# A softmax denominator's inverse: VectorE's reciprocal replaced by Ln and Exp on ScalarE, in an eight-core transformer layer

## The chip, the cores and the metric

One Trainium2 chip, all 8 of its cores. Each core runs the same program on its own 2 of 16 sequences; no core talks to another. The metric is the device time of the slowest core, in microseconds (us). Two runs of the kernel before gave 9357.95 and 9133.69 us, median 9245.82 us.

## The reference

A transformer layer with a layer norm behind each half, in float32, on x of 16 x 2048 x 2048. What matters here is the attention, and in it the division by the sum of the exponentials (the rest of the layer is cut short):

```python
q = einsum('bsd,ed->bse', x, Wq)...; k = ...; v = ...      # 16 heads of 128
q = q * cos + rotate_half(q) * sin                         # k the same
scores = einsum('bhqd,bhkd->bhqk', q, k) / sqrt(128)
scores = where(causal, scores, finfo.min)
attn = softmax(scores, axis=-1)                            # exp(s) / sum(exp(s))
out = einsum('bhqk,bhkd->bhqd', attn, v) ... @ Wo.T
x = layernorm(x + out)
x = layernorm(x + (relu(relu(x @ W1.T + b1) @ W2.T + b2) @ W3.T + b3))
```

## The kernel before

The program goes through five stages for each of a core's two sequences (b = 0, 1), with a barrier of all engines ahead of the attention and behind it: Q, K and V projections (matmuls L384 and L433), attention (L498, L545, L554), output projection with the first layer norm (L660), and the three feed-forward layers (L724, L754, L790) with the second. Every instruction of an engine stands in the order in which the Python code emits it. The helpers `C.pe`, `C.act` and `C.dve` append to an engine's list, with semaphore waits written out by hand; nothing reorders them.

In the attention one unit of work is a block of 512 queries (index `q4`, 0 to 3) of one head, so there are 16 x 4 units for each sequence and 128 in all. A unit has `nci = 4*q4 + 4` blocks of 128 keys, that is 4, 8, 12 and 16 blocks for `q4` of 0, 1, 2 and 3. For each block, `emit_st` puts down:

- on TensorE the scores, 128 keys x 512 queries, into one of four PSUM banks (L498);
- on ScalarE `exp(score * scale - 16)`, PSUM to SBUF in bf16 (L512);
- on VectorE, in the last four blocks of the unit, which hold the diagonal, a memset of the masked columns (L509) and a multiplication of 128 x 128 by the triangular mask (L519).

`emit_lav` then puts down two matmuls that read the exponentials: a column of ones, which adds them up into row 0 of `l_bank` (L545), and V, which accumulates 128 x 512 in `avb` (L554). Scores run three blocks ahead of them. With `q4 = 0` all four blocks are diagonal ones, so that L545 waits for VectorE's mask from its first block on; with `q4` of 1 or more the first blocks need ScalarE alone.

At the end of a unit the sums in row 0 of `l_bank` are inverted. VectorE does it in four steps on 1 x 512 elements, of which the last three split the result into two bf16 numbers:

```python
t_rc = C.dve(... e.reciprocal(linv_sb[0:1, :], l_bank.t[0:1, :]) ...)     # L575
t_hi = C.dve(... linv_hi <- linv_sb ...)                                  # L579
t_hf = C.dve(... linv_hif <- linv_hi ...)                                 # L581
t_lo = C.dve(... linv_lo <- linv_sb - linv_hif ...)                       # L583
```

What uses them is put off by one unit. `flush_tail[0]()` (L574) emits the tail of the unit before: two matmuls that spread the inverse over 128 rows (L592, L595), a copy of it to SBUF (L600) and the multiplication with `avb` (L606), both on VectorE, and the store of the product (L612), which ScalarE's queue issues. So the order on VectorE at the end of unit n is L600 and L606 of unit n-1, then L575 to L583 of unit n, then the masks of unit n+1. On ScalarE the order is the exponentials of unit n, the store of unit n-1 (which waits for L606), then the exponentials of unit n+1.

Of the kernel before, what the change touches and what calls it, by code (L numbers as in the profile page):

```python
# [10 lines left out]
AF = mybir.ActivationFunctionType  # L11
# [126 lines left out]
def build_program(cfg, debug=False):  # L138
# [47 lines left out]
    with st:  # L186
        C = Ctx(nc, st)
        s_pe, s_act, s_dve = C.sems["pe"], C.sems["act"], C.sems["dve"]
# [3 lines left out]
                for nm in ("x0", "x1", "wq", "wk", "wv", "wo", "w1", "w2", "w3")}  # L192
# [32 lines left out]
        consts = nc.alloc_sbuf_tensor("consts", [128, 4], F32)  # L225
# [7 lines left out]
        linv_sb = nc.alloc_sbuf_tensor("linv_sb", [1, 512], F32)  # L233
        linv_hi = nc.alloc_sbuf_tensor("linv_hi", [1, 512], BF16)
        linv_hif = nc.alloc_sbuf_tensor("linv_hif", [1, 512], F32)
# [9 lines left out]
        banks = [Bank(st.enter_context(nc.psum_tensor(f"pb{i}", [128, 512], F32)))  # L245
                 for i in range(8)]

        NEGC, SCL, EPSC = 0, 1, 2
        cvec = lambda i: consts[:, i:i + 1]

        C.dve(lambda e: e.memset(consts[:, NEGC:NEGC + 1], -CSHIFT), inc=False)
        C.dve(lambda e: e.memset(consts[:, SCL:SCL + 1], SCALE), inc=False)
        C.dve(lambda e: e.memset(consts[:, EPSC:EPSC + 1], EPS), inc=False)
        C.dve(lambda e: e.memset(ones_cb[:, :], 1.0), inc=False)
        C.dve(lambda e: e.memset(ones_rb[:, :], 1.0), inc=False)
        C.dve(lambda e: e.memset(ones_rf[:, :], 1.0))
# [7 lines left out]
                       waits=[tk_ini])  # L264
# [89 lines left out]
        for b in range(B):  # L354
            if b == 0:
                C.barrier()
            for dc in range(ND):
                tk_xT = C.ld(m_xt, AA[:, xT_o + dc * S: xT_o + (dc + 1) * S],
                             xb_hbm.ap()[b, :, dc * 128:(dc + 1) * 128],
                             waits=[tk_xcast[b], (s_pe, prev_f_last)], transpose=True)  # L360
# [8 lines left out]
            for (wsrc, wtok, dst) in ((wq_bf, tk_wq, qT_hbm), (wk_bf, tk_wk, kT_hbm)):  # L369
                for h in range(H):  # L370
# [6 lines left out]
                        waits=[wtok, pan_freed[bi], (s_pe, prev_f_last)])  # L377
                    for sb in range(NSB):
                        bk = banks[it % 2]
                        for dc in range(ND):  # L380
                            wl = []
                            if dc == 0:
# [6 lines left out]
                                waits=wl, inc=(dc == ND - 1))  # L389
# [9 lines left out]
                            waits=[(s_pe, tmm), (s_dve, tmp_done[r]), tk_ini,  # L399
                                   (s_act, prev_ln_sqrt), (m_sout, m_sout.n)])  # L400
# [7 lines left out]
                            waits=[(s_dve, tc), stage_store[r]])  # L408
# [4 lines left out]
                                               waits=[(s_dve, td)])  # L413
# [5 lines left out]
            for eb in range(NEB):  # L419
# [6 lines left out]
                    waits=[tk_wv, vp_freed[bi], (s_pe, prev_f_last)])  # L426
                for sc in range(NS):
                    bk = banks[2 + (it % 2)]
                    for dc in range(ND):
                        wl = []  # L430
                        if dc == 0:
# [6 lines left out]
                            waits=wl, inc=(dc == ND - 1))  # L438
# [5 lines left out]
                        waits=[(s_pe, tmm), vs_store[r]])  # L444
# [8 lines left out]
                                        waits=[(s_act, tev)])  # L453
# [13 lines left out]
            linv_used = None  # L467
            rep_prev = None
# [4 lines left out]
            for h in range(H):  # L473
# [13 lines left out]
                for q4 in range(NSB):  # L487
                    nci = 4 * q4 + 4
                    avb = av_banks[iav[0] % 2]
                    l_bank = l_banks[iav[0] % 2]  # L490
# [76 lines left out]
                    tav_last = None  # L567
                    for ci in range(3, nci):
                        emit_st(ci)
                        tav_last = emit_lav(ci - 3)  # L570
                    tav_last = emit_lav(nci - 3)
                    tav_last = emit_lav(nci - 2)
                    tav_last = emit_lav(nci - 1)
                    flush_tail[0]()  # L574
                    t_rc = C.dve(lambda e, l_bank=l_bank: e.reciprocal(  # L575
                        linv_sb[0:1, :], l_bank.t[0:1, :]),
                                 waits=[(s_pe, tav_last), (s_dve, linv_used),
                                        (s_pe, rep_prev)])
                    t_hi = C.dve(lambda e: e.tensor_copy(linv_hi[0:1, :], linv_sb[0:1, :]),  # L579
                                 waits=[(s_dve, t_rc)])  # L580
                    t_hf = C.dve(lambda e: e.tensor_copy(linv_hif[0:1, :], linv_hi[0:1, :]),  # L581
                                 waits=[(s_dve, t_hi)])
                    t_lo = C.dve(lambda e: e.tensor_sub(linv_lo[0:1, :], linv_sb[0:1, :],  # L583
                                                        linv_hif[0:1, :]),
                                 waits=[(s_dve, t_hf)])
                    linv_used = t_lo
                    l_bank.free = (s_dve, t_rc)

                    def tail(l_bank=l_bank, avb=avb, t_lo=t_lo, tav_last=tav_last,
                             q4=q4, h=h, b=b):  # L590
# [41 lines left out]
            for g in range(NS // 4):  # L632
# [5 lines left out]
                    waits=[otg_freed[gb]])  # L638
                otg = AB[:, otg_o + gb * H * 512: otg_o + (gb + 1) * H * 512]
                for eb in range(NEB):  # L640
# [6 lines left out]
                        waits=[tk_wo, wop_freed[wb_i]])  # L647
                    for si in range(4):
# [5 lines left out]
                                          waits=[xc_freed[xr]])  # L654
                        bk = banks[itb % 6]
                        for h in range(H):
                            wl = []
                            if h == 0:
# [6 lines left out]
                                waits=wl, inc=(h == H - 1))  # L665
# [240 lines left out]
```

How the kernel before makes its waits and increments, by code:

```python
    def emit(self, eng, fn, waits=(), inc=None, inck=1):  # L76
        lst = self.ops[eng]
        wt = self.waited[eng]
        for w in waits:
            if w is None:
                continue
            s, v = w
            if v is None or v <= 0:
                continue
            if wt.get(s.name, 0) >= v:
                continue
            wt[s.name] = v
            lst.append(lambda e, s=s, v=v: e.wait_ge(s.h, v))
        if inc is not None:
            inc.n += inck
            tok = inc.n
            def run(e, fn=fn, inc=inc, k=inck):
                fn(e).then_inc(inc.h, k)
            lst.append(run)
            return tok
        lst.append(fn)
        return None
# [28 lines left out]
    def barrier(self):  # L128
        toks = [(s, s.n) for s in self.all_sems if s.name not in self.no_barrier]
        for e in self.ENGS:
            for s, v in toks:
                if v <= 0 or self.waited[e].get(s.name, 0) >= v:
                    continue
                self.waited[e][s.name] = v
                self.ops[e].append(lambda eng, s=s, v=v: eng.wait_ge(s.h, v))
# [691 lines left out]
        def final_waits(e):  # L827
            for s, v in fin:
                if v > 0:
                    e.wait_ge(s.h, v)
```

## Time and profile before

| | us |
|---|---|
| two runs | 9133.69, 9357.95 (median 9245.82) |
| profiled execution | 9160.52 |
| its slowest core, first to last instruction (the span) | 9158.9 |
| spans of the eight cores | 9042.0 to 9158.9 |
| attention stages of the slowest core | about 1822 to 2740 and 5848 to 6744 |

The profile is of the slowest core, core 1, and times in it count from the start of its span. "Busy" is time in which an engine ran an instruction; a row of the timeline that ends in brackets says how long the engine stood idle before it and what ended that. [...]

### The profile page before, as it was taken

What the parts mean: (1) busy time and instruction counts of PE and PEld (TensorE: products, weight loads), DVE (VectorE), ACT (ScalarE), POOL (GpSimd) and SP (SyncE); (2) the same over time, 40 slices, a digit from 0 to 9 for tenths busy, and PEclk for the clock granted to TensorE, in tenths of its full rate; (3) what the DMA queues carried; (4) which work ended last, traced back from release to release, by engine and by line L of the source; (5) the groups of instructions that cost most, each with busy time, mean ns of one, the idle gap of its engine ahead of it and who ended that gap; (6) DMA issues with size and microseconds to landing.
All of it is one profiled execution on the core that took longest, in us unless ns stands there. A gap on an engine that the chain in (4) does not pass through costs nothing.

```text
span 9158.9 us, 76236 instructions; the slowest of 8 cores (9042.0 to 9158.9 us)
## 1 busy us (share of the span) xinstructions
PE 6904.8 (75%) x28800; PEld 2716.3 (30%) x28800; DVE 2147.2 (23%) x3399; ACT 1432.9 (16%) x2116; POOL 33.5 (0%) x68
## 2 busy tenths in 40 slices
PE   0000099977776698998989799877766798989898
PEld 0000044411112243443434344311122343434343
DVE  0000087055542201000000474255532001010101
ACT  0000000144440110101010000344420101011010
POOL 0000000000000000000000000000000000000000
PEclk9999999978778899999999899877788999999999
DMA  9999922211116645444444422111136544444444
GB/s 116 110 109 111 119 76 87 67 37 38 37 46 212 180 149 164 149 157 160 172 150 162 120 78 82 54 44 37 38 128 204 156 159 157 159 152 149 168 146 155
DMA packets 423222, 1097.90 MB, mean 120 GB/s; under 512 B 228433, under 2 KB 277713, under 8 KB 367825
## 3 DMA queue, kind: packets, MB, share of 16 engines
q1 hardware_dynamic: 282066, 824.54, 27.4%
q0 software_dynamic: 8704, 134.22, 12.6%
q10 hardware_dynamic: 132096, 134.25, 4.5%
q8 instruction: 240, 3.93, 0.2%
q14 instruction: 116, 0.95, 0.0%
HBM read 1025.78 MB, written 268.44 MB: 141 GB/s over the span
## 4 chain that ended last, share of the span: by engine, by line
PE 63%; SPq 13%; DMA 13%; DVE 5%; issue 2%; another core or an unknown queue 1%; ACT 1%; ACTq 0%; DVEq 0%; POOLq 0%
PE pb L754 18%; SPq L112 13%; PE pb L384 10%; PE pb L724 8%; PE pb L790 6%; PE pb L554 5%; PE pb L545 5%; DMA arena_a<-w_bf 5%; PE pb L433 5%; DMA arena_b<-w_bf 4%; DMA arena_b<-wo_bf 3%; PE pb L660 3%; PE pb L498 2%; DVE linv_sb L575 1%
## 5 line engine op out<-in xcount | busy, mean ns | idle before, releaser
L384 PE MATMUL pb<-arena_a,arena_b 128*128 128x512 bf16 x4096 | 892.0, 381 | 1205.6 <-DMA arena_b<-wq_bf 1198.3
L754 PE MATMUL pb<-arena_a,arena_b 128*128 128x512 bf16 x8192 | 1770.0, 379 | 8.7 <-ACT arena_a L731 7.4
L724 PE MATMUL pb<-arena_b 128*128 128x512 bf16 x4096 | 931.4, 385 | 264.3 <-DMA arena_b<-w_bf 217.7
L754 PEld LDWEIGHTS pb<-arena_a,arena_b 128*128 128x128 bf16 x8192 | 800.4, 98 | 978.3 <-issue 15.8
L512 ACT ACTIVATE arena_b<-pb,consts 128x512 bf16<-128x512 f32 (+3 forms) x1280 | 854.1, 714 | 923.4 <-DVE ot_stage L606 460.7
L790 PE MATMUL pb<-arena_a,arena_b 128*128 128x512 bf16 x4096 | 937.4, 388 | 80.9 <-DMA arena_a<-w_bf 79.1
L803 DVE TENSOR_TENSOR farena<-pb,xc_sb 128x512 f32<-128x512 f32 x128 | 88.5, 691 | 3767.9 <-PE pb L796 3767.9
L384 PEld LDWEIGHTS pb<-arena_a,arena_b 128*128 128x128 bf16 x4096 | 402.2, 98 | 1694.8 <-issue 1216.5
L545 PE MATMUL pb<-arena_b,ones_cb 128*1 128x512 bf16 x1280 | 555.9, 434 | 376.4 <-ACT arena_b L512 188.8
L660 PE MATMUL pb<-arena_b 128*128 128x512 bf16 x2048 | 498.8, 409 | 252.7 <-DMA arena_b<-wo_bf 221.6
L724 PEld LDWEIGHTS pb<-arena_b 128*128 128x128 bf16 x4096 | 393.7, 99 | 800.8 <-issue 374.3
L790 PEld LDWEIGHTS pb<-arena_a,arena_b 128*128 128x128 bf16 x4096 | 398.5, 100 | 589.7 <-issue 155.0
L554 PE MATMUL pb<-arena_b 128*128 128x512 bf16 x1280 | 570.6, 446 | 0.0
L498 PE MATMUL pb<-arena_b 128*128 128x512 bf16 x1280 | 501.4, 444 | 21.4 <-DMA arena_b<-v_hbm 21.4
L397 DVE TENSOR_TENSOR farena<-pb,sin_sb 64x512 f32<-64x512 f32 x256 | 177.3, 693 | 1171.3 <-PE pb L384 1170.6
L433 PE MATMUL pb<-arena_b,arena_a 128*128 128x512 bf16 x2048 | 442.7, 379 | 1.0 <-ACT v_stage L442 1.0
L575 DVE RECIPROCAL linv_sb<-pb 1x512 f32<-1x512 f32 x128 | 426.8, 3335 | 4.9 <-PE pb L554 4.9
L761 ACT ACTIVATE arena_b<-pb,b2t_sb 128x512 bf16<-128x512 f32 x256 | 175.9, 687 | 1603.4 <-PE pb L754 1603.4
L323 ACT ACTIVATE farena<-farena 128x2048 f32<-128x2048 f32 x64 | 122.2, 1910 | 1814.1 <-DVE farena L803 1053.3
L545 PEld LDWEIGHTS pb<-arena_b,ones_cb 128*1 128x1 bf16 x1280 | 101.2, 79 | 966.1 <-issue 966.1
L660 PEld LDWEIGHTS pb<-arena_b 128*128 128x128 bf16 x2048 | 210.7, 104 | 541.7 <-issue 337.6
L731 ACT ACTIVATE arena_a<-pb,b1t_sb 128x512 bf16<-128x512 f32 x256 | 175.8, 687 | 862.6 <-PE pb L724 853.4
(53 smaller groups left out, 2271.6 us busy)
## 6 DMA issues: line engine op xcount, KB each, us to landing
arena_b<-w_bf SPq DMA_DIRECT2D x256, 1024.0 KB, 4.9
arena_b<-w_bf SPq DMA_DIRECT2D x256, 512.0 KB, 3.4
arena_a<-w_bf SPq DMA_DIRECT2D x32, 4096.0 KB, 15.2
arena_b<-wo_bf SPq DMA_DIRECT2D x32, 2048.0 KB, 10.9
w_bf<-w2T POOLq DMA_DIRECT2D x8, 4096.0 KB, 787.3
xc_sb<-x SPq DMA_DIRECT2D x128, 256.0 KB, 5.2
y_hbm<-farena ACTq DMA_DIRECT2D x32, 1024.0 KB, 8.9
xc_sb<-y_hbm SPq DMA_DIRECT2D x128, 256.0 KB, 4.6
```

Of the source, the lines that this page charges most:

```text
L112: fn = lambda e: e.dma_start(out, in_, transpose=True)
L384: tmm = C.pe(lambda e, bk=bk, off=off, dc=dc, sb=sb: e.matmul(bk.t[:, :], AB[:, off + dc * 128: off + (dc + 1) * 128], AA[:, xT_o + dc * S ...
L433: tmm = C.pe(lambda e, bk=bk, off=off, dc=dc, sc=sc: e.matmul(bk.t[:, :], AA[:, xT_o + dc * S + sc * 128: xT_o + dc * S + sc * 128 + 128], ...
L498: tmm = C.pe(lambda e, bk=bk, ci=ci, q4=q4, qb=qb, kb=kb: e.matmul(bk.t[:, :], kb[:, ci * 128:(ci + 1) * 128], qb[:, q4 * 512:(q4 + 1) * 512],
L512: te = C.act(lambda e, bk=bk, ao=ao, j=max(j, 0): e.activation(AB[:, ao + 128 * j: ao + 512], bk.t[:, 128 * max(j, 0):], AF.Exp, bias=cvec ...
L545: C.pe(lambda e, ci=ci, ar=ar, l_bank=l_bank: e.matmul(l_bank.t[0:1, :], ones_cb[:, :], AB[:, ab_o + ar * 512: ab_o + (ar + 1) * 512], sta ...
L554: tav = C.pe(lambda e, ci=ci, ar=ar, avb=avb, vb=vb: e.matmul(avb.t[:, :], vb[:, ci * 128:(ci + 1) * 128], AB[:, ab_o + ar * 512: ab_o + ( ...
L575: t_rc = C.dve(lambda e, l_bank=l_bank: e.reciprocal(linv_sb[0:1, :], l_bank.t[0:1, :]), waits=[(s_pe, tav_last), (s_dve, linv_used), (s_p ...
L660: tmm = C.pe(lambda e, bk=bk, h=h, si=si, woff=woff, otg=otg: e.matmul(bk.t[:, :], otg[:, h * 512 + si * 128: h * 512 + si * 128 + 128], A ...
L724: tmm = C.pe(lambda e, bk=bk, woff=woff, dc=dc: e.matmul(bk.t[:, 0:STILE], AB[:, woff + dc * 128: woff + (dc + 1) * 128], AB[:, yT_o + dc ...
L754: tmm = C.pe(lambda e, bk=bk, woff=woff, ec=ec: e.matmul(bk.t[:, 0:STILE], AB[:, woff + ec * 128: woff + (ec + 1) * 128], AA[:, h1_o + ec ...
L790: C.pe(lambda e, bk=bk, woff=woff, ec=ec, si=si: e.matmul(bk.t[:, :], AB[:, h2_off(ec) + si * 128: h2_off(ec) + si * 128 + 128], AA[:, wof ...
```

## The change

The inverse of the sum l is no longer VectorE's reciprocal but exp(-ln(l)), in two ScalarE activations of 1 x 512 elements: Ln from PSUM into `linv_hif` (which serves as scratch and is overwritten by L581 later), then Exp with a scale of -1, read from a new column of `consts`, into `linv_sb`. VectorE's three remaining steps wait for ScalarE in place of VectorE. Both activations stand in ScalarE's queue where the code stood for VectorE: behind the store that `flush_tail` issues, ahead of the exponentials of the next unit. `l_bank` is now freed by Ln.

```diff
-        NEGC, SCL, EPSC = 0, 1, 2
+        NEGC, SCL, EPSC, NEG1 = 0, 1, 2, 3
...
+        C.dve(lambda e: e.memset(consts[:, NEG1:NEG1 + 1], -1.0), inc=False)
...
                     flush_tail[0]()
-                    t_rc = C.dve(lambda e, l_bank=l_bank: e.reciprocal(
-                        linv_sb[0:1, :], l_bank.t[0:1, :]),
-                                 waits=[(s_pe, tav_last), (s_dve, linv_used),
-                                        (s_pe, rep_prev)])
+                    t_ln = C.act(lambda e, l_bank=l_bank: e.activation(
+                        linv_hif[0:1, :], l_bank.t[0:1, :], AF.Ln),
+                        waits=[(s_pe, tav_last), (s_pe, rep_prev),
+                               (s_dve, linv_used)])
+                    t_rc = C.act(lambda e: e.activation(
+                        linv_sb[0:1, :], linv_hif[0:1, :], AF.Exp,
+                        scale=consts[0:1, NEG1:NEG1 + 1]),
+                        waits=[(s_act, t_ln)])
                     t_hi = C.dve(lambda e: e.tensor_copy(linv_hi[0:1, :], linv_sb[0:1, :]),
-                                 waits=[(s_dve, t_rc)])
+                                 waits=[(s_act, t_rc)])
...
                     linv_used = t_lo
-                    l_bank.free = (s_dve, t_rc)
+                    l_bank.free = (s_act, t_ln)
```

The line numbers of the changed kernel are higher by 1 up to this place and by 5 behind it: L512 becomes L513, L579 becomes L584, L606 becomes L611.

ScalarE, from the last two exponentials of a unit with `q4 = 3` into the next head's `q4 = 0`, before:

```order
L512 ACTIVATE arena_b<-pb,consts 128x256 [waits sm_pe]
L512 ACTIVATE arena_b<-pb,consts 128x128 [waits sm_pe]
L119 DMA oT_hbm<-ot_stage 128x512 [waits sm_dve]
L512 ACTIVATE arena_b<-pb,consts 128x512 [waits sm_pe]
L512 ACTIVATE arena_b<-pb,consts 128x384 [waits sm_pe]
```

and now:

```order
L513 ACTIVATE arena_b<-pb,consts 128x256 [waits sm_pe]
L513 ACTIVATE arena_b<-pb,consts 128x128 [waits sm_pe]
L119 DMA oT_hbm<-ot_stage 128x512 [waits sm_dve]
L576 ACTIVATE linv_hif<-pb 1x512 [waits sm_pe]
L580 ACTIVATE linv_sb<-linv_hif,consts 1x512 [waits sm_act]
L513 ACTIVATE arena_b<-pb,consts 128x512 [waits sm_pe]
L513 ACTIVATE arena_b<-pb,consts 128x384 [waits sm_pe]
```

The two new activations stand between the store and the first exponential of the next unit, in all 128 units.

VectorE at the same place, from the tail's multiplication to the masks of `q4 = 0`, before:

```order
L606 TENSOR_TENSOR ot_stage<-pb,lrep_sb 128x512 [waits sm_dve,sm_sot0]
L575 RECIPROCAL linv_sb<-pb 1x512
L579 CAST linv_hi<-linv_sb 1x512 [waits sm_dve]
L581 CAST linv_hif<-linv_hi 1x512 [waits sm_dve]
L583 TENSOR_TENSOR linv_lo<-linv_sb,linv_hif 1x512 [waits sm_dve]
L519 TENSOR_TENSOR arena_b<-arena_b,masks_sb 128x128 [waits sm_act]
```

and now:

```order
L611 TENSOR_TENSOR ot_stage<-pb,lrep_sb 128x512 [waits sm_dve,sm_sot0]
L584 CAST linv_hi<-linv_sb 1x512 [waits sm_act]
L586 CAST linv_hif<-linv_hi 1x512 [waits sm_dve]
L588 TENSOR_TENSOR linv_lo<-linv_sb,linv_hif 1x512 [waits sm_dve]
L520 TENSOR_TENSOR arena_b<-arena_b,masks_sb 128x128 [waits sm_act]
```

The reciprocal is gone, and the first cast waits for ScalarE; the masks of the next unit still stand behind the three short steps. TensorE's order is the same.

## Rows read from the trace of the kernel before

**Rows 1.** The page: TensorE's busy share, and its granted clock in 40 slices.

```profile
PE 6904.8 (75%) x28800; PEld 2716.3 (30%) x28800; DVE 2147.2 (23%) x3399; ACT 1432.9 (16%) x2116; POOL 33.5 (0%) x68
...
PEclk9999999978778899999999899877788999999999
```

**Rows 2.** Busy time of each engine, then clock, in the second attention stage.

```profile
5848.00:6744.00 896.00, 696.36 (x2045) 149.21 (x2044) 491.61 (x832) 426.87 (x641) 0.00 (x0) 0.80 0.10 35
```

**Rows 3.** What L545's matmul waited for (us, times), whole span.

```profile
  ACT arena_b L512: 188.8, 98
  DVE arena_b L519: 187.5, 32
```

**Rows 4.** Timeline from `q4 = 3` into `q4 = 0`: start, length, instruction, idle before.

```profile
2320.43 1.04 PE L498 MATMUL pb<-arena_b 128*128 128x512 bf16 x4
...
2321.46 0.69 DVE L606 TENSOR_TENSOR ot_stage<-pb,lrep_sb 128x512 bf16<-128x512 f32 x1 [0.17 <-DVE lrep_sb L600]
2322.07 3.33 DVE L575 RECIPROCAL linv_sb<-pb 1x512 f32<-1x512 f32 x1
2322.23 0.33 ACTq L119 DMA_DIRECT2D oT_hbm<-ot_stage  x1
2322.66 2.15 ACT L512 ACTIVATE arena_b<-pb,consts 128x512 bf16<-128x512 f32 x4 [4.66 <-DVE ot_stage L606]
2325.51 0.41 DVE L579 CAST linv_hi<-linv_sb 1x512 bf16<-1x512 f32 x1
...
2327.16 0.20 DVE L519 TENSOR_TENSOR arena_b<-arena_b,masks_sb 128x128 bf16<-128x128 bf16 x1
...
2327.61 0.59 PE L545 MATMUL pb<-arena_b,ones_cb 128*1 128x512 bf16 x1 [6.15 <-DVE arena_b L519]
```

**Rows 5.** Timeline from `q4 = 2` into `q4 = 3`.

```profile
2302.53 1.04 PE L498 MATMUL pb<-arena_b 128*128 128x512 bf16 x4
...
2304.76 1.45 ACT L512 ACTIVATE arena_b<-pb,consts 128x512 bf16<-128x512 f32 x2 [4.66 <-DVE ot_stage L606]
...
2305.79 0.38 PE L545 MATMUL pb<-arena_b,ones_cb 128*1 128x512 bf16 x1 [2.23 <-ACT arena_b L512]
```

**Rows 6.** Timeline, TensorE's first L545 in a unit with `q4 = 1`.

```profile
2336.06 0.59 PE L545 MATMUL pb<-arena_b,ones_cb 128*1 128x512 bf16 x1 [1.38 <-ACT arena_b L512]
```

**Rows 7.** ScalarE's groups by shape: count, then busy us and mean ns.

```profile
L512 ACT ACTIVATE arena_b<-pb,consts 128x512 bf16<-128x512 f32 x896 | 648.3, 779 | 836.6 <-DVE ot_stage L606 460.7 <-PE pb L498 361.2
...
L731 ACT ACTIVATE arena_a<-pb,b1t_sb 128x512 bf16<-128x512 f32 x256 | 175.8, 687 | 862.6 <-PE pb L724 853.4 <-DVE farena L343 9.2
...
L442 ACT CAST v_stage<-pb 128x512 bf16<-128x512 f32 x128 | 75.0, 586 | 854.8 <-PE pb L433 832.8 <-DMA v_hbm<-v_stage 20.9 <-ACT v_stage L442 1.2
...
L512 ACT ACTIVATE arena_b<-pb,consts 128x128 bf16<-128x128 f32 x128 | 58.7, 459 | 28.1 <-PE pb L498 28.1
...
L338 ACT ACT_TABLE_LOAD x2 | 2.6, 1283 | 2.3 <-DVE stats L335 2.3
```

**Rows 8.** Timeline of ScalarE: a cast, and the store that waits for it.

```profile
1701.77 0.59 ACT L442 CAST v_stage<-pb 128x512 bf16<-128x512 f32 x1 [2.87 <-PE pb L433]
1702.43 0.37 ACTq L119 DMA_DIRECT2D v_hbm<-v_stage  x1
```

**Rows 9.** As rows 2: 8 us behind three of the 2.23 us waits.

```profile
2235.23:2243.23 8.00, 8.00 (x24) 1.54 (x24) 4.09 (x8) 6.77 (x10) 0.00 (x0) 0.81 0.00 0
2249.58:2257.58 8.00, 8.00 (x29) 1.88 (x30) 3.22 (x4) 7.73 (x12) 0.00 (x0) 1.00 0.00 0
2290.08:2298.08 8.00, 8.00 (x19) 1.27 (x19) 3.32 (x5) 5.66 (x9) 0.00 (x0) 0.61 0.00 1
```

**Rows 10.** The same behind waits of 3.81 and 3.61 us (L790) and 3.32 us (L660).

```profile
3995.45:4003.45 8.00, 8.00 (x30) 3.33 (x31) 0.00 (x0) 0.00 (x0) 0.00 (x0) 0.79 0.05 16
...
8509.81:8517.81 8.00, 8.00 (x25) 3.12 (x26) 0.00 (x0) 0.00 (x0) 0.00 (x0) 0.66 0.03 11
7087.18:7095.18 8.00, 8.00 (x38) 3.64 (x39) 1.38 (x2) 0.00 (x0) 0.00 (x0) 1.00 0.20 40
```

## The prediction

> **What bounds the kernel now.** I read the page first. TensorE is busy 75% of the span and no other engine over 23%, and its granted clock dips in two places, slices 9 to 14 and again near 28 [rows 1]. Those are the two attention stages, and the change touches nothing else. In the second of them, 896 us long, TensorE is busy 696 us, VectorE 492 and ScalarE 427, at a mean clock of 0.80 [rows 2]. So no engine fills the stage: it is a chain from engine to engine that repeats in every unit, and the question is who is late at each hand-over.
>
> The waits of L545, the first matmul that reads exponentials, say it. Over both stages it stood idle 188.8 us for ScalarE's L512, 98 times, and 187.5 us for VectorE's mask L519, 32 times [rows 3]. These are the starts of units: 96 units have `q4` of 1 or more, 32 have `q4 = 0`.
>
> The timeline shows the two patterns. Into `q4 = 0` [rows 4]: L606 ends at 2322.15, VectorE then runs the 3.33 us reciprocal, the three short steps from 2325.51 on, and the first mask at 2327.16. TensorE has had its four score matmuls done since 2321.47 and waits 6.15 us. ScalarE, which started at 2322.66, was done long before. Here the reciprocal is on the path. Into `q4 = 3` [rows 5]: ScalarE's store waits for L606, the first exponential starts at 2304.76, and L545 follows it after 2.23 us of waiting. VectorE's reciprocal runs beside all this and nobody wants its result for a whole unit. [...]
>
> **The change, part by part.**
>
> *The two activations.* No row has a 1 x 512 activation, so I take 128 x 512 ones, since the lanes work side by side. Three groups differ in how many operands are read from a column in SBUF rather than being constants: L442 none, 586 ns; L731 a bias, 687; L512 bias and scale, 779 [rows 7]. Ln takes none: 0.59. Exp takes the scale -1: 0.69. Exp waits for Ln on its own engine; the nearest row is a store that starts 0.07 us behind the cast it waits for (1701.77 + 0.59, then 1702.43) [rows 8], and VectorE's cast starts 0.11 behind the reciprocal [rows 4]. I take 0.15. The exponential behind it starts 0.11 before its predecessor ends (two take 1.45, one 0.78) [rows 5, 7]. So the next unit's exponentials are late by 0.59 + 0.15 + 0.69 - 0.11 = 1.32 us.
>
> *Units with `q4` of 1 or more.* What is queued behind the new instructions on ScalarE is exactly what L545 waits for. TensorE has nothing else to do meanwhile, and behind the start it sets the pace (29 matmuls in 8 us [rows 9], so 0.83 us for the three of a block, against 1.45 - 0.78 = 0.67 for an exponential), so nothing is caught up. The whole 1.32 us is lost: 96 x 1.32 = 126.7 us.
>
> *Units with `q4 = 0`.* Ln starts where the first exponential started, 2322.66, and ends at 2323.25; Exp runs from 2323.40 to 2324.09. The first cast starts 0.15 later, at 2324.24 instead of 2325.51. From there the masks follow as before, so the wait of 6.15 us shrinks by 1.27. The first exponential, now done at about 2324.8, is still ahead of the mask at 2325.9, so VectorE stays last. That is 3.33 us taken off VectorE and only 1.27 off the path, since ScalarE's two steps start 0.6 us later than the reciprocal did and take 1.4. It holds for the 30 units with a unit before them: -38.1 us. The last unit of each sequence ends in the same chain: -2.5 us.
>
> *Order alone gives* 126.7 - 38.1 - 2.5 = +86 us.
>
> *The clock.* The waits of 2.23 us grow to 3.55. Of six such waits between 2235 and 2362, the 8 us behind them had a mean clock of 1.00 twice, about 0.80 three times and 0.61 once, mean 0.835; one of each is shown [rows 9]. No attention wait is near 3.55 us, but the feed-forward has six waits for DMA of 3.6 to 3.9 us, and behind them it was 0.79 or 0.80 five times and 0.66 once, mean 0.77; one of each is shown [rows 10]. In the attention 8 us hold 29 matmuls at clock 1.00 and 24 at 0.81 [rows 9]: 5 x 8/29 = 1.4 us for 0.2 of clock. So one unit of clock over 8 us is worth 6.9 us, a loss of 0.065 costs 0.45 us, and 64 units (`q4` of 2 and 3) have this wait: +29 us. [...]
>
> *Nothing:* the added memset (once), the waits on two semaphores that were passed earlier, `l_bank` freed by Ln (the bank is wanted two units later), the 3.33 us on VectorE in the 96 units where they ran beside other work.
>
> *Bounds.* Each activation lies between 0.46 (the 128-column L512) and 0.78, the step between them between 0.07 and 0.3. Low: the exponentials are late by 0.88, `q4 = 0` gains 1.79, and the order gives 96 x 0.88 - 32 x 1.79 = +27. High: 1.75 and 0.82, +142. The clock term lies between 0 (behind the 3.32 us wait it stayed at 1.00 [rows 10]) and a clock of 0.61 behind every wait: 0.225 x 6.9 x 64 = +99.
>
> *Table loads.* A load of ScalarE's tables takes 1283 ns, and L338's 64 square roots, between other functions, show only two in the whole span [rows 7]. If Ln and Exp lay in different tables, every unit would have two. [...] The changed program as compiled holds no more loads than the one before. So I put nothing, and keep the other case as a rival.
>
> Sum: 86 + 29 = +115 us on the profiled execution's 9160.5 (its span of 9158.9 and 1.6 around it) gives 9276 us, +1.3%. That execution lies near the lower of the two runs (9133.69) and below their median of 9245.82; I count from it, since the durations are its own.
>
> **The rivals.**
>
> *The clock pays more (slower by over 2%).* [...] For it: 0.61 and 0.66 occur, and the stage has a mean of 0.80 with shorter waits. Against: most waits of 3.6 to 3.9 us cost one stretch, 0.79. It decides from a mean clock of about 0.61 behind the 64 waits.
>
> *Table reloads (slower by over 2%).* Two loads a unit, 2.57 us: 96 x 2.57 = 247 and 30 x 2.57 = 77 on top of 115 give +439, 9600 us. Against it is what stands above.
>
> *The shorter `q4 = 0` wait keeps the clock (not slower).* This is the one place where the path gets shorter. At 4.88 us of wait instead of 6.15 the clock might not fall. Then the ten matmuls from there to the next copy (eight of the unit, two of the tail), which start at 0.59 us [rows 4] against 0.38 [rows 5], save 10 x 0.21 = 2.1 us, and the unit behind, which begins at 0.59 too [rows 6], one stretch or a little more, 1.8 us; 30 x 3.9 = 117 us. With the clock term of the other waits at 0 that is 86 - 117 = -31, 9130 us, -0.3%. Against it: waits of 3.6 to 3.9 us lost the clock six times out of six, and it decides only if a wait of 4.9 us is short enough.
>
> *It does not do what it says:* if a lane's pace made 1 x 512 activations dearer, both patterns would be worse; this lies in the bounds.
>
> **How the numbers follow.** Forecast 72%, the clock rival 15%, table reloads 3%, the kept clock 5%, and 5% for what I do not see. The likeliest case gives 9276 us. Its own low end is +27, but both activations at a quarter of the columns is unlikely; I take +45, 9205 us. At the top I go to just past the clock rival, 9400. A measurement of this kernel tells about 2% from no change, 183 us here. Slower by over that are the clock rival, the table rival and a little of the forecast's upper bounds: 0.20. Faster by over 2% has no case: 0.02. Within 2%: 0.78.
>
> **What would show it.** In the profile of the changed kernel: L576 about 590 ns and L580 about 690; L545's wait for L513 near 2.70 us with `q4 = 1` and 3.55 with `q4` of 2 and 3, so 310 us in total over 96 units instead of 188.8; its wait for the mask L520 near 4.9 us, about 150 us in total instead of 187.5; the attention stages each some 55 us longer at a mean clock of 0.78 to 0.80, all other stages the same; no more table loads than before. I am wrong if the first exponential starts as early as before, if ACT_TABLE_LOAD appears 256 times, if the clock behind the 3.55 us waits is near 0.6 or near 1.0, or if the stages outside the attention move.

## The result, and the profile after

The changed kernel has a median of 9410.73 us over 11 runs (9243.07 to 9797.73), the kernel before, on the same chips, 9378.47 us over 10 runs (9104.11 to 9778.43). The ratio is 1.0165, interval 1.0122 to 1.0209: the change makes the kernel slower by 1.65%. In about every other execution of either kernel one die ran at a lower clock and took one to six hundred us longer; the medians above contain them (9410.73 is itself such an execution), while the ratios, and the times and stage lengths quoted for the experiments, are of executions and dies without that.

The profiled execution took 9309.96 us. Its waits are those forecast. The first matmul that reads exponentials (L546 now) stood idle for, in us and times over the whole span:

```profile
  ACT arena_b L513: 317.7, 98
  DVE arena_b L520: 147.7, 35
```

Against 188.8 and 187.5 us [rows 3] that is +128.9 for ScalarE and -39.8 for VectorE's mask, +89 in sum. The two new activations, ScalarE's groups by shape with busy us and mean ns of one:

```profile
L580 ACT ACTIVATE linv_sb<-linv_hif,consts 1x512 f32<-1x512 f32 x128 | 92.2, 720 | 12.1 <-ACT linv_hif L576 0.4
...
L576 ACT ACTIVATE linv_hif<-pb 1x512 f32<-1x512 f32 x128 | 75.0, 586 | 690.3 <-DVE ot_stage L611 476.4 <-PE pb L499 206.9 <-PE pb L555 7.0
```

Ln is 586 ns on one partition, as L442 is on 128 [rows 7], and Exp 720. VectorE shows the same for 64 and 128 partitions before (L397 and L403, 693 and 692 ns). The timeline from `q4 = 3` into `q4 = 0`, which answers to [rows 4]:

```profile
2305.91 0.69 DVE L611 TENSOR_TENSOR ot_stage<-pb,lrep_sb 128x512 bf16<-128x512 f32 x1 [0.17 <-DVE lrep_sb L605]
2306.68 0.33 ACTq L119 DMA_DIRECT2D oT_hbm<-ot_stage  x1
2307.16 0.59 ACT L576 ACTIVATE linv_hif<-pb 1x512 f32<-1x512 f32 x1 [4.71 <-DVE ot_stage L611]
2307.84 0.72 ACT L580 ACTIVATE linv_sb<-linv_hif,consts 1x512 f32<-1x512 f32 x1
2308.47 2.10 ACT L513 ACTIVATE arena_b<-pb,consts 128x512 bf16<-128x512 f32 x4
2308.66 0.42 DVE L584 CAST linv_hi<-linv_sb 1x512 bf16<-1x512 f32 x1 [2.06 <-ACT linv_sb L580]
...
2310.31 0.20 DVE L520 TENSOR_TENSOR arena_b<-arena_b,masks_sb 128x128 bf16<-128x128 bf16 x1
...
2310.77 0.58 PE L546 MATMUL pb<-arena_b,ones_cb 128*1 128x512 bf16 x1 [4.86 <-DVE arena_b L520]
```

The exponentials start 1.31 us behind Ln's start (2307.16 to 2308.47); forecast 1.32. Exp follows Ln after 0.09 us, the cast follows Exp after 0.10. The wait for the mask is 4.86 us; forecast 4.88. In units with `q4 = 3` the wait for ScalarE is 3.56 us (forecast 3.55), with `q4 = 1` 2.71 (forecast 2.70):

```profile
6013.05 0.58 PE L546 MATMUL pb<-arena_b,ones_cb 128*1 128x512 bf16 x1 [3.56 <-ACT arena_b L513]
```

```profile
2320.54 0.59 PE L546 MATMUL pb<-arena_b,ones_cb 128*1 128x512 bf16 x1 [2.71 <-ACT arena_b L513]
```

What was not forecast is the clock. The profile gives it as a share of full speed. In the kernel before, all windows of 0.2 us between 2314 and 2318 read 1.00, with matmuls of 512 columns of 0.38 and 0.39 us in them, and all of 0.4 us between 2327.6 and 2335.6 read 0.50, with matmuls of 0.58 to 0.61 us up to 2331.8; "half clock" is the second, and a value in between is taken as the mean of such stretches. The second attention stage, from its first to its last tail multiplication, before (first fence) and after: length, busy time of TensorE, its weight loads, VectorE, ScalarE and GpSimd with their instructions, granted clock, DMA.

```profile
5863.00:6740.00 877.00, 684.16 (x2008) 146.29 (x2006) 482.81 (x813) 419.57 (x628) 0.00 (x0) 0.80 0.10 35
```

```profile
5931.00:6897.00 966.00, 720.64 (x1967) 147.66 (x2006) 279.08 (x750) 497.74 (x754) 0.00 (x0) 0.75 0.09 32
```

VectorE lost 204 us of work and ScalarE gained 78, and the stage is 89 us longer. TensorE is busy 36 us more with the same matmuls (41 records are missing): they ran at half clock more often (0.75 against 0.80 in the mean). From the start of the first tail multiplication to that of the last, in every core's trace, the two stages are 880 and 877 us long before, as means over the eight cores, and 964 and 965 after: +85 and +88, +173 us in all. The stretch between them and the one behind them were 10 and 15 us shorter; they differ by as much between profiled executions of the other kernels here. 173 - 25 = 148 us is the 1.65%. In what follows "stages" is this pair of lengths.

The clock in the 8 us behind two of the 3.56 us waits, which answers to [rows 9]:

```profile
6013.05:6021.05 8.00, 8.00 (x20) 1.35 (x21) 0.80 (x2) 5.76 (x9) 0.00 (x0) 0.63 0.00 0
6057.70:6065.70 8.00, 8.00 (x20) 1.37 (x21) 1.11 (x4) 5.88 (x9) 0.00 (x0) 0.65 0.00 0
```

Of the 60 waits of this length in the trace none is followed by more than 0.67, and their mean is 0.64. For before the prediction took 0.835 from six waits; all 64 of them in that trace give 0.82. The number of table loads did not change:

```profile
L339 ACT ACT_TABLE_LOAD x2 | 2.6, 1283 | 2.3 <-DVE stats L336 2.3
...
L443 ACT ACT_TABLE_LOAD x1 | 1.3, 1283 | 1592.9 <-PE pb L434 1592.9
L513 ACT ACT_TABLE_LOAD x1 | 1.3, 1283 | 9.7 <-PE pb L499 9.7
```

Four, and none at L576 or L580: the 128 pairs of Ln and Exp ran with no load between. The load at L443 is ahead of ScalarE's first instruction (1592.94 us), those at L339 ahead of the first square root behind the exponentials of each sequence (2897.5 and 6994.7), the one at L513 ahead of the first exponential behind square roots (5914.24), each 1283 ns.

### The profile page after: what moved, and what is told of

It reads as the page before. It is cut to its first block, busy times and chain, and to the rows that moved or that the text cites. A ratio compares the mean times of both kernels' runs of the same rounds, so it can differ in the third digit from the quotient of the medians.

```text
span 9308.4 us, 76172 instructions; the slowest of 8 cores (9204.5 to 9308.4 us)
## 1 busy us (share of the span) xinstructions
PE 6941.8 (75%) x28225; PEld 2714.9 (29%) x28800; DVE 1734.5 (19%) x3272; ACT 1590.7 (17%) x2372; POOL 33.5 (0%) x68
## 4 chain that ended last, share of the span: by engine, by line
PE 63%; SPq 13%; DMA 12%; DVE 4%; ACT 3%; issue 3%; another core or an unknown queue 2%; ACTq 1%; DVEq 0%; POOLq 0%
PE pb L759 18%; SPq L112 13%; PE pb L385 9%; PE pb L729 8%; PE pb L795 6%; PE pb L546 5%; PE pb L555 5%; DMA arena_a<-w_bf 5%; PE pb L434 5%; DMA arena_b<-wo_bf 3%; DMA arena_b<-w_bf 3%; PE pb L665 3%; PE pb L499 2%; ACT arena_b L513 2%
## 5 line engine op out<-in xcount | busy, mean ns | idle before, releaser
L729 PE MATMUL pb<-arena_b 128*128 128x512 bf16 x4014 | 924.8, 385 | 239.2 <-DMA arena_b<-w_bf 174.6
L546 PE MATMUL pb<-arena_b,ones_cb 128*1 128x512 bf16 x1280 | 587.4, 459 | 474.2 <-ACT arena_b L513 317.7
L513 ACT ACTIVATE arena_b<-pb,consts 128x512 bf16<-128x512 f32 (+3 forms) x1280 | 856.5, 704 | 251.5 <-PE pb L499 223.9
L665 PE MATMUL pb<-arena_b 128*128 128x512 bf16 x2007 | 500.3, 412 | 257.1 <-DMA arena_b<-wo_bf 232.6
L555 PE MATMUL pb<-arena_b 128*128 128x512 bf16 x1240 | 585.2, 472 | 0.0
L499 PE MATMUL pb<-arena_b 128*128 128x512 bf16 x1239 | 517.2, 469 | 28.6 <-DMA arena_b<-v_hbm 21.0
L546 PEld LDWEIGHTS pb<-arena_b,ones_cb 128*1 128x1 bf16 x1280 | 101.2, 79 | 1107.9 <-issue 1107.9
L520 DVE TENSOR_TENSOR arena_b<-arena_b,masks_sb 128x128 bf16<-128x128 bf16 x512 | 107.4, 210 | 1164.9 <-ACT arena_b L513 1158.3
```

The costliest lines, as they stand in the source:

```text
L499: tmm = C.pe(lambda e, bk=bk, ci=ci, q4=q4, qb=qb, kb=kb: e.matmul(bk.t[:, :], kb[:, ci * 128:(ci + 1) * 128], qb[:, q4 * 512:(q4 + 1) * 512],
L513: te = C.act(lambda e, bk=bk, ao=ao, j=max(j, 0): e.activation(AB[:, ao + 128 * j: ao + 512], bk.t[:, 128 * max(j, 0):], AF.Exp, bias=cvec ...
L546: C.pe(lambda e, ci=ci, ar=ar, l_bank=l_bank: e.matmul(l_bank.t[0:1, :], ones_cb[:, :], AB[:, ab_o + ar * 512: ab_o + (ar + 1) * 512], sta ...
L555: tav = C.pe(lambda e, ci=ci, ar=ar, avb=avb, vb=vb: e.matmul(avb.t[:, :], vb[:, ci * 128:(ci + 1) * 128], AB[:, ab_o + ar * 512: ab_o + ( ...
L665: tmm = C.pe(lambda e, bk=bk, h=h, si=si, woff=woff, otg=otg: e.matmul(bk.t[:, :], otg[:, h * 512 + si * 128: h * 512 + si * 128 + 128], A ...
L729: tmm = C.pe(lambda e, bk=bk, woff=woff, dc=dc: e.matmul(bk.t[:, 0:STILE], AB[:, woff + dc * 128: woff + (dc + 1) * 128], AB[:, yT_o + dc ...
```

## The experiments

Each stands with its edit, the expectation on record, and the stages' lengths beside it. L-numbers below are those of the kernel in question.

### The pair added, the reciprocal kept

```diff
 flush_tail[0]()
+t_d1 = C.act(activation(FA[0:1, 512:1024], FA[0:1, 0:512], AF.Ln))
+C.act(activation(FA[0:1, 1024:1536], FA[0:1, 512:1024], AF.Exp, scale=-1), waits=[(s_act, t_d1)])
 t_rc = C.dve(reciprocal(linv_sb, l_bank))
```

> The kernel before, with an Ln and an Exp of 1 x 512 added to ScalarE's queue where the changed kernel has them, on scratch data that nothing reads; VectorE keeps its reciprocal. Theory A (the loss is the delay of ScalarE's exponentials at the start of units with q4 of 1 or more, plus the clock that falls more behind longer waits): L545's waits for L512 become 2.7 us (q4 = 1) and 3.56 us (q4 of 2 and 3), the 6.15 us wait for the mask stays, and the two attention stages together grow by 96 x 1.33 = 128 us plus about 87 of clock, +215 us over before (+2.3%), more than the change itself. Rival B (the loss is that VectorE's casts now wait for ScalarE, a longer chain from the sums to the split inverse): nothing waits for the added pair, 0 to +20 us.

Stages 965 and 965 us, +173 over before; times 9236.96 to 9283.24 us against 9105.34 beside them. L547's waits, on core 6:

```profile
  ACT arena_b L514: 330.2, 98
  DVE arena_b L521: 187.2, 32
```

The waits are near theory A's, that for the mask included, and rival B is refuted: VectorE's chain was left as it was, and the time is the changed kernel's. But 215 us were expected and 173 came, with 141 us more of waiting than before, where the changed kernel has 89 more. So the clock's part is not a fixed price for a wait: it was smaller here by about as much.

### Ln alone added

```diff
 flush_tail[0]()
+C.act(activation(FA[0:1, 512:1024], FA[0:1, 0:512], AF.Ln))
 t_rc = C.dve(reciprocal(linv_sb, l_bank))
```

> The kernel before with only the Ln of 1 x 512 added to ScalarE's queue, on scratch data. The delay is 0.49 to 0.59 us, waits 1.9 and 2.8 us. [...] If the clock's loss comes in one step above 3 us of wait, +53 alone (+0.6%).

Stages 898 and 894, +35 us; waits for ScalarE 238.0 us (+49), for the mask 188.6; ratio 1.0094, interval 1.0047 to 1.0141, of which more than half lies outside the attention, in two runs. Forecast were 96 x 0.55 = +53 us for the order, and +86 with a term for the clock. Both were too high: the waits grew by 50 us in all and the stages by 35, so the clock took nothing here and gave some 14 us back. Over all cores the 8 us behind the 2.69 us waits had 0.82 with `q4 = 2` and 0.81 with `q4 = 3`, where before had 0.75 and 0.90 behind 2.23 us: about the same on average.

### A copy in place of the reciprocal

```diff
-t_rc = C.dve(reciprocal(linv_sb, l_bank))
+t_rc = C.dve(tensor_copy(linv_sb, l_bank))
```

> The kernel before, with the reciprocal replaced by a copy of the sums (0.42 us in place of 3.33), so the division is left out. Theory A: only the 32 starts of q4 = 0 shorten, from 6.15 to 3.2 us, 30 x 2.9 = -87 us and -6 at the two ends, -93 us (-1.0%), and the clock behind the shorter wait stays low, so no more than 20 us come on top. Rival C (the wait of q4 = 0 is so long that it alone pulls the clock down; shortened, it gives the clock back): -93 and another 60 to 120 us, -1.7% to -2.3%. Rival B: the reciprocal was on the path in every unit, -128 x 2.9 = -371 us.

Stages 852 and 853, -52 us. The wait for the mask fell from 187.5 to 105.6 us in total (3.5 us each), for ScalarE 180.3. Two new waits, for VectorE's casts, are 6.4 us. So the path gave up some 84 us and the time 52, where theory A had 93: the stage's clock was 0.79, a little under before's 0.80 although it idled less. Rival C had it the wrong way round, and rival B, the reciprocal on the path everywhere, is out by a factor of seven.

### The pair for `q4 = 3` only, and for the others only

```diff
+if q4 == 3:      # the other kernel: q4 != 3
     t_ln = C.act(... AF.Ln); t_rc = C.act(... AF.Exp ...)
+else:
+    t_rc = C.dve(reciprocal ...)
```

> ScalarE's Ln and Exp only for the units with q4 = 3, whose successor has q4 = 0; VectorE's reciprocal for the other 96. Theory A: the good part of the change alone. The wait for the mask is 4.88 us, the waits for exponentials stay at 1.38 and 2.23, and the stages together shorten by 32 x 1.27 = 41 us (-0.45%), with 20 us either way from the clock. Rival B (a cast that waits for ScalarE costs more than its 0.15 us): 0 or slower.

> ScalarE's Ln and Exp only for the 96 units with q4 of 0 to 2, VectorE's reciprocal for q4 = 3. Theory A: the bad part of the change alone. Waits for exponentials 2.7 and 3.56 us, the wait for the mask 6.15 as before, stages together +128 for the order and about +87 for the clock, +215 us (+2.3%), and with e3 it adds up to the change's +173 us in the attention stages. Rival: if the clock's part hangs on the q4 = 0 wait and not on the lengthened ones, only about +128 us.

The first: stages 860 and 864, -33 us; runs of 9049.10 to 9098.11 against 9105.34 beside them. Its waits are 193.7 for ScalarE and 149.2 for the mask. The second: stages 966 and 966, +175 us; runs of 9253.21 to 9271.45; waits 340.8 and 184.5. The first came out as expected, the second 40 us under theory A's +215. The change is a good part and a bad part, and they can be had apart: the starts behind the `q4 = 3` units gain, the other 96 lose. The parts give +142 together and the change +173, so again some 30 us hang on how the waits follow each other and not on their number.

### TensorE kept busy in the waits

```diff
 def emit_st(ci):
+    for _ in range(8 if ci == 3 else 0):
+        C.pe(matmul(bk.t, kb[ci], qb[q4], start=True, stop=True))   # same as below, same bank
     tmm = C.pe(matmul(bk.t, kb[ci], qb[q4], start=True, stop=True))
```

> The changed kernel, with the score matmul of each unit's fourth block put down eight times more ahead of the real one, into the same bank (1024 more matmuls, the result is the same). They run in TensorE's wait at a unit's start, so L546 cannot start earlier or later by order: its start hangs on ScalarE or VectorE. Theory A (the part of the loss that the order does not explain is TensorE's clock, which falls behind the longer idle wait): the idle wait with q4 of 2 and 3 shrinks from 3.56 to about 1.9 us, the granted clock of the attention stages rises from 0.76 to 0.85 or more, and the stages shorten by at least the 87 us that the change lost to the clock, to 9150 us or under. Rival D (the clock follows something else in the stage, as the share of one-column matmuls, and the waits only coincide): clock within 0.02 of 0.76 and the time the same or, by the added matmuls at the low clock, 0 to 60 us more.

> The same eight added matmuls a unit in the kernel before. Theory A: its 2.23 us waits shrink to about 0.6 us and stop costing clock, the 6.15 us wait becomes 4.5 and still costs it; clock of the stages from 0.80 to 0.88 or so, -60 to -120 us. Rival D: same clock, 0 to +60 us. Against e5 it is still faster by the order's 86 us, within 30.

In the changed kernel the stages fell from 964 and 965 to 871 and 871, in the kernel before from 880 and 877 to 817 and 816, though each has 1024 more matmuls. The second stage of one core, changed kernel with the added matmuls, then the kernel before with them:

```profile
5778.00:6649.00 871.00, 743.37 (x2502) 195.25 (x2500) 278.30 (x750) 487.90 (x754) 0.00 (x0) 0.92 0.11 35
```

```profile
5793.00:6610.00 817.00, 716.62 (x2504) 193.95 (x2502) 479.25 (x814) 411.02 (x628) 0.00 (x0) 0.95 0.11 38
```

The granted clock went from 0.75 to 0.92 and from 0.80 to 0.95. With TensorE at work in the waits the clock was 0.17 and 0.15 higher, so its idle time there is what lowered it in these two kernels, and rival D is refuted: the one-column matmuls are the same ones. The second expectation's -60 to -120 us came as -124. The distance between the two kernels shrank from 173 us to 109, nearer to the 89 us of waiting by which they differed.

### The inverse put down later

```diff
 for ci in range(3, nci):
     emit_st(ci)
+    if ci == (3, 3, 5, 9)[q4] and pend_inv[0]:
+        pend_inv[0]()                  # Ln, Exp, L584, L586, L588 of the unit before
+        pend_inv[0] = None
     tav_last = emit_lav(ci - 3)
```

> The changed kernel with the whole inverse (Ln, Exp and VectorE's three steps) put down later, inside the next unit, behind its block 3, 3, 5 or 9 for q4 of 0, 1, 2 and 3, where ScalarE runs ahead of TensorE. Theory A (it is the place in ScalarE's queue that costs, not the work): waits for exponentials back to 1.4 and 2.23 us, the wait for the mask down to about 2.6 us, and a new wait of up to 2 us of the tail's L597 for the split inverse in units with q4 = 0; order -30 x 1.9 = -58 us over before, time 9000 to 9120 us, faster than both kernels. Rival E (the 1.3 us on ScalarE cannot be hidden anywhere in the unit, since ScalarE with its exponentials is near its limit there): about the changed kernel's time, within 40 us.

Stages 821 and 822, -113 us, twice what was expected; ratio 0.986, interval 0.9813 to 0.9907. L547 waits for ScalarE at all starts and hardly for VectorE, and the feared wait of the tail's first matmul is 11 us in total. TensorE's groups by shape, with busy us, mean ns, and the idle time before:

```profile
L547 PE MATMUL pb<-arena_b,ones_cb 128*1 128x512 bf16 x1280 | 554.4, 433 | 269.4 <-ACT arena_b L514 265.3 <-DVE arena_b L521 3.8
...
L608 PE MATMUL pb<-linv_hi,ones_rb 1*128 1x512 bf16 x128 | 56.1, 438 | 11.3 <-DVE linv_lo L596 11.2
```

188.8 + 187.5 us of waiting became 265.3 + 3.8 + 11.2, 96 us less. The whole gain lies at one start: from the first L547 of a `q4 = 3` unit to that of the next `q4 = 0` unit it takes 17.27 us on average instead of 21.10, because the masks no longer stand behind the inverse, while the three other distances are 8.24, 11.72 and 14.79 us instead of 8.22, 11.52 and 14.81. So the same two activations cost almost nothing where ScalarE runs ahead of TensorE, and rival E is refuted. The expectation had put 1.6 us on the tail in each of 30 units, and that did not come. One rival was not run: VectorE's reciprocal put down later in the same way. It is therefore not shown that the gain needs Ln and Exp at all; the later place alone may give it.

### Both, with eight and with four added matmuls

> e7 (the inverse put down later) and the eight added score matmuls of e5 together. Theory A: both gains hold, since one takes away the delays and the long mask wait and the other the idle time that the remaining 1.4 to 2.6 us waits leave: stages from e7's 821 us to 770 to 790, granted clock there from 0.82 to above 0.92, time -1.8% to -2.8% against before in undisturbed runs. Rival: with e7's short waits the clock has little left to give, and the 1024 added matmuls cost what they bring: within 20 us of e7.

> As e9 with four added matmuls a unit in place of eight. They fill 0.85 us of the 1.4 to 2.6 us waits in place of 1.7. Theory A: stages between e7's 821 us and e9's, nearer to e9's if a wait of about 1.4 us is short enough for the clock, clock 0.86 to 0.94. Rival: no gain below eight, within 10 us of e7's stages.

With eight, stages 802 and 799, clock 0.96, ratio 0.9852 (0.9798 to 0.9906); with four, 803 and 799, clock 0.92. Eight miss the expected 770 to 790: the stages are 20 us under the inverse put down later alone, and in the time of the whole kernel there is no difference that shows, as the rival had it. The tail's first matmul, which waited 11 us in total with the inverse put down later alone, now waits for the split inverse where the expectation for that kernel had feared it:

```profile
L614 PE MATMUL pb<-linv_hi,ones_rb 1*128 1x512 bf16 x128 | 52.0, 406 | 54.3 <-DVE linv_lo L602 54.3
```

Four, expected nearer to eight than to none, do in the stages what eight do; this rests on the stages of one profiled execution.

### The column of ones made 128 wide

```diff
-ones_cb = nc.alloc_sbuf_tensor("ones_cb", [128, 1], BF16)
+ones_cb = nc.alloc_sbuf_tensor("ones_cb", [128, 128], BF16)
...
-C.pe(matmul(l_bank.t[0:1, :], ones_cb[:, :], ...))
+C.pe(matmul(l_bank.t[:, :], ones_cb[:, :], ...))
```

> The changed kernel with the column of ones that adds up the exponentials made 128 columns wide, so that L546 writes the sums to all 128 rows (only row 0 is read; its stream of 512 columns is as long as before). It asks why the clock stayed low for longer behind the 3.56 us waits (5.7 of 8 us) than behind the feed-forward's waits of 3.6 to 3.9 us (3.4), which the prediction took as its measure. If the one-column matmuls of the attention hold the clock down after a wait, the 5.7 us fall to 3.4 to 4.5 us and the stages shorten by 20 to 50 us each. If it is the pattern of waits alone, the stages stay within 10 us of 964 us.

The changed kernel's stages fell from 964 and 965 to 821 and 824, far beyond the 20 to 50 us; ratio to the kernel before 0.9886 (0.9819 to 0.9953). Most of it has nothing to do with the clock. TensorE's timeline at full clock, kernel before, then with wide ones:

```profile
2314.00 0.38 PE L545 MATMUL pb<-arena_b,ones_cb 128*1 128x512 bf16 x1
2314.31 0.39 PE L554 MATMUL pb<-arena_b 128*128 128x512 bf16 x1
2314.53 0.38 PE L498 MATMUL pb<-arena_b 128*128 128x512 bf16 x1
2314.84 0.38 PE L545 MATMUL pb<-arena_b,ones_cb 128*1 128x512 bf16 x1
```

```profile
2313.82 0.38 PE L546 MATMUL pb<-arena_b,ones_cb 128*128 128x512 bf16 x1
2314.04 0.38 PE L555 MATMUL pb<-arena_b 128*128 128x512 bf16 x1
2314.26 0.38 PE L499 MATMUL pb<-arena_b 128*128 128x512 bf16 x1
2314.47 0.38 PE L546 MATMUL pb<-arena_b,ones_cb 128*128 128x512 bf16 x1
```

Start to start, the matmul ahead of the one-column one and that one itself take 0.31 us, and 0.22 when the ones are wide: 0.84 us a block against 0.65. Over 640 blocks of a stage that is up to 122 us. The weight loads (PEld) in the same stretches show where the 0.09 us at each change to or from one column lie, before first and then with wide ones:

```profile
2313.99 0.08 PEld L545 LDWEIGHTS pb<-arena_b,ones_cb 128*1 128x1 bf16 x1 [0.42 <-issue]
2314.30 0.10 PEld L554 LDWEIGHTS pb<-arena_b 128*128 128x128 bf16 x1 [0.23 <-issue]
2314.32 0.10 PEld L498 LDWEIGHTS pb<-arena_b 128*128 128x128 bf16 x1
```

```profile
2314.04 0.10 PEld L499 LDWEIGHTS pb<-arena_b 128*128 128x128 bf16 x1
2314.26 0.10 PEld L546 LDWEIGHTS pb<-arena_b,ones_cb 128*128 128x128 bf16 x1
2314.47 0.10 PEld L555 LDWEIGHTS pb<-arena_b 128*128 128x128 bf16 x1
```

With wide ones each load starts as the matmul before its own starts (L499's at 2314.04 with L555, its own matmul at 2314.26), so it is hidden behind that matmul. With the column, the loads of L545 and of L554 start 0.01 us before their own matmuls, 0.30 us behind the start of the matmul before. That TensorE waits for them is an estimate from these times: the 0.09 us at each change are about the 0.08 to 0.10 us of such a load. The load of one column is not slower (79 ns against 98), it is only not hidden; why it is not, no run here shows. The clock behind two of the 3.56 us waits, which are still there:

```profile
6016.93:6024.93 8.00, 8.00 (x30) 3.36 (x31) 0.80 (x2) 7.39 (x12) 0.00 (x0) 0.80 0.01 2
6042.82:6050.82 8.00, 8.00 (x26) 2.84 (x26) 3.08 (x10) 4.09 (x7) 0.00 (x0) 0.71 0.00 0
```

0.80 and 0.71, and 0.76 as the mean of 77 (some of them now at `q4 = 1`), in place of 0.64. The next kernel asks how much of the change's own loss is left then.

> The kernel before with the column of ones made 128 columns wide. It asks how much of e10's gain has to do with the change. e10's stages fell from 964 to 822 us; the blocks' pace went from 0.84 to 0.65 us, which has nothing to do with the clock's fall. If the change's loss is order (43 us a stage) and clock (42 us a stage), and the clock's part hangs on the one-column matmuls, before with wide ones has stages of 822 - 43 = 779 us, within 15. If the clock's part stays, 822 - 85 = 737 us. If ScalarE (0.67 us a block) is the bound in the long units once TensorE needs 0.65, the order's part changes too, and the stages lie outside 737 to 795.

Stages 764 and 761, against 821 and 824: the change costs 120 us with wide ones and 173 with narrow ones. The order's 44 us a stage are there (the first waits of the units are 90 us longer in the changed kernel with wide ones than in the kernel before with them), and some 16 of the 42 us of clock. So most of the clock's part, not all of it, goes with the wide ones; 764 is just inside the expected 764 to 794, 761 just outside. The times are 8851.79 and 8874.34 us.

> e7 (the inverse put down later) with the wide ones. Theory A: e7's 58 us a stage against before and the faster blocks both hold: stages 700 to 760 us, time about 8750 to 8850 us, 3% to 4.5% under before and under every other kernel here. Rival: with TensorE at 0.65 us a block, ScalarE at 0.67 is the bound, so the 1.3 us pair cannot be hidden in units with q4 of 2 and 3: 64 x 1.3 = 83 us come back, stages 745 to 800 us.

Stages 754 and 755, which both expected ranges contain; times 8828.22 to 8870.86 us, ratio 0.972, interval 0.9684 to 0.9757, the lowest here. Against the wide ones alone the later inverse gains 16 us in the stages, not 113, which the times of the whole kernel don't tell apart. L547's waits in it:

```profile
  ACT arena_b L514: 363.6, 252
  DVE arena_b L521: 23.7, 19
```

252 times instead of 127: ScalarE is now what TensorE waits for inside the units too, and these waits, about 95 us behind the units' starts, speak for the rival and its 83. This version beats both kernels, most of it by the wide ones.

## Why the prediction was right or wrong

- **The direction and the mechanism held.** VectorE's 3.33 us were on the path at the 30 starts of `q4 = 0` that have a unit before them and at the end of each sequence, and the pair on ScalarE lengthened the wait of the 96 other starts. The kernel with the pair added and the reciprocal kept, and the two halves of the change, show both parts alone.
- **The term "96 x 1.32".** Forecast +126.7 us, measured +128.9 of waiting. Exp was taken at 0.69 and the step to it at 0.15 us; they are 0.72 and 0.09, and the errors cancel.
- **The term for `q4 = 0`.** Forecast -38.1 - 2.5, measured -39.8.
- **The base is the step that failed in the time.** The sum was put on one profiled execution's 9160.5 us, 1% below the median then known and 218 us (2.3%) below the 9378 us that the kernel before had over ten runs. In absolute time 9410.73 us lies 135 us above the forecast of 9276 and 11 us above the range's end of 9400, and this comes from the base and not from the terms of the change: with the clock term as measured below the same sum gives 9331 us, and against the profiled execution of the changed kernel, 9309.96 us, the forecast is only 34 us short. A range for a median of this kernel should have been put on the median, or been wide enough to reach what half of its runs take. In relation the forecast was +1.3% and the result +1.65%.
- **The clock term is the step that failed in the change.** Forecast 29 us, measured 173 - 89 = 84. It was worked out as (0.835 - 0.77) x 6.9 x 64. What went wrong is the 0.77, borrowed from the feed-forward's DMA waits of the same length [rows 10]. Behind the attention's 3.56 us waits the clock is 0.64; in the same formula that is 86 us, and 89 + 86 = 175 against 173 measured. The bound that was given for this term, 0 to +99, did hold it.
- **What does fix the clock behind a wait is only partly shown.** The wait's length does not: before has 0.75 behind the 2.23 us waits of `q4 = 2` and 0.90 behind those of `q4 = 3`. The column of ones has a part in it: with wide ones the 3.56 us waits had a mean of 0.76 behind them. Whether the width itself, the quicker pace or the shorter distance between waits does that was not separated, and the feed-forward's waits differ from the loop's in all of these.
- **The rivals.** "The clock pays more" was the nearest: its 99 us for the 64 waits, the upper bound of the clock term, is within 15 us of what was found, and the result stayed under 2%. The 9400 us at the range's top also count in 45 us of clock in `q4 = 1`, a term that no run shows; there some 8 came. Table reloads did not come. "The shorter wait keeps the clock" is refuted twice: behind the wait of 4.86 us in the timeline above the clock over 8 us was 0.50, as behind 6.15 us before, and behind the 3.5 us waits of the copy it was 0.50 or 0.51 on every core's mean.
- **Still open:** why the clock's price of a pattern of waits does not add up over its parts: 84 us in the changed kernel, 173 - 141 = 32 with the pair added beside the reciprocal, and 32 the wrong way with the copy.

The traces do show where it lies. The table has the mean time in us from the first L545 of a unit until TensorE's next first wait begins, which is the same list of matmuls in every row, so that a difference is clock, but for 0.1 us or so of small waits. The last column is the sum of the four differences to before, times 32.

| kernel | `q4 = 0` | 1 | 2 | 3 | clock's part |
|---|---|---|---|---|---|
| before | 6.86 | 9.28 | 12.58 | 14.92 | |
| changed | 6.83 | 9.52 | 13.22 | 16.72 | +85 |
| pair added (two cores) | 5.60 | 9.30 | 13.11 | 16.67 | +33 |
| pair not for `q4 = 3` | 5.41 | 9.25 | 13.06 | 16.64 | +23 |
| copy for the reciprocal | 6.88 | 8.94 | 13.16 | 15.66 | +32 |

Two thirds of what the change pays, 32 x 1.80 = 58 us, is paid in the units with `q4 = 3`. Where the 6.15 us wait for the mask was kept, the pair costs the same there and the `q4 = 0` units give 40 to 46 us back. The 8 us behind such a wait, before and with the pair not for `q4 = 3`:

```profile
6014.35:6022.35 8.00, 7.06 (x14) 1.25 (x14) 3.25 (x7) 0.59 (x1) 0.00 (x0) 0.50 0.02 7
```

```profile
6002.42:6010.42 8.00, 5.48 (x14) 1.11 (x14) 2.16 (x6) 1.17 (x2) 0.00 (x0) 0.71 0.05 16
```

The wait and the ten matmuls behind it are the same, and over all cores the clock behind it is 0.50 in 205 of 216 cases before and 0.71 or more in 237 of 240 in the other kernel. So neither the length of a wait nor the work that follows it fixes the clock; what lies before the wait, or the moment at which it falls, has a part. The median head (four units) takes 61.4 us in the changed kernel and also in both kernels with the pair that kept the 6.15 us wait, although the waiting in both stages together grew by 89 us in the one and by 141 and 149 in the others. Why they fall into the same step was not tested.

## What to carry to other kernels

Moving a slow operation to an idle engine helps only if its queue is late there too: ask, for each place of the queue, who waits for the instruction behind. Here the same two activations made the kernel 1.65% slower at a unit's start and, with VectorE's steps, 1.4% faster than before when put down a few exponentials later; whether the reciprocal in that later place would have done as well was not run. When a change lengthens TensorE's waits in a repeated pattern, the price of its clock cannot be borrowed from waits of the same length in another stage: here that gave a third of what was paid. And a forecast of a median is put on the median, not on the one execution that was profiled.

## What the runs showed of the hardware

- A column of ones as weights between 128-column weights costs TensorE 0.09 us at each change, 0.19 us a block, although its matmul streams the same 512 columns: its weight load and the one behind it start only 0.01 us before their matmuls, where with 128 columns a load starts 0.22 us before its own. Making it 128 wide took 116 us off each attention stage of the kernel before (880 to 764).
- Eight matmuls that repeat one of the kernel's own, put into each first wait of a unit, raised the granted clock of the attention from 0.80 to 0.95 and took 124 us off, with 1024 more matmuls.
- An Exp of 1 x 512 whose scale is read from SBUF takes 720 ns, Ln of the same size with constants 586, as the cast of 128 x 512 (L442, 586): one partition cost what 128 did.
- Waits of 2.7 us inside the loop left the stage's clock as 2.23 us ones did (0.81 and 0.80); waits of 3.56 us took it to 0.75.
- The same 6.15 us wait with the same matmuls behind it was followed by a clock of 0.50 over 8 us in one kernel and of 0.71 in another.
